# A decoder on one core: the second cross attention's outputs are finished a batch later, and the feed-forward weights are loaded and summed during it

## The chip, the cores and the metric

The kernel runs on one core of a Trainium2 chip. The metric is the device time of one execution in microseconds (us), less is better. PE is TensorE, DVE is VectorE, ACT is ScalarE, POOL is GpSimd, and SP is the engine whose queue issues all DMA transfers here. Each engine runs its own instruction stream in order; streams meet only at semaphores.

## The reference, cut to what matters

Six layers run one after the other on x of 32 batches x 256 tokens x 256 features, all float32, each followed by a residual addition and a layer norm. The change is in the last two:

```python
# 5: cross attention to ctx (32 x 77 x 256), 16 heads of 16
Q = _split_heads(query @ Wq.T + bq)
K = _split_heads(key @ Wk.T + bk)
V = _split_heads(value @ Wv.T + bv)
attn = jax.nn.softmax(jnp.einsum('bhqd,bhkd->bhqk', Q, K) / jnp.sqrt(jnp.float32(HEAD_DIM)), axis=-1)
out = jnp.einsum('bhqk,bhkd->bhqd', attn, V).transpose(0, 2, 1, 3).reshape(B, S, H * Dh)
x = _layernorm(x + (out @ Wo.T + bo))
# 6: feed-forward with ternary weights and 8-bit activations, inner width 1024
scale = 1.0 / jnp.clip(jnp.mean(jnp.abs(w)), 1e-05)              # of each weight matrix
wq = jnp.clip(jnp.round(w * scale), -1.0, 1.0) / scale
gate = jax.nn.silu(_bitlinear(x, w_gate)); up = _bitlinear(x, w_up)
x = _layernorm(x + _bitlinear(gate * up, w_down))
```

So the scale of a weight matrix needs the sum of the absolute values of all its elements before one element can be rounded.

## The kernel before, in words

`decoder` runs six stages in a row. Each opens a `Stage`, which allocates its buffers and semaphores, writes one instruction stream per engine, and ends with a barrier of all engines; a stage's last store has to land before the next stage starts. Results go through DRAM between stages (`act`).

**`cross_attention_in_halves`** (stage "xa", the second use of cross attention; the first is another function and unchanged) works through 32 batches. A batch has four units u = 0..3, (token tile t, head half c) with 8 heads x 77 context positions = 616 columns each. For each unit PE makes scores, DVE takes maxima (L1597) and subtracts (L1598), ACT takes exponentials (`expo`, L1416), DVE sums and takes the reciprocal (`sums`, L1605 and L1606), POOL multiplies (`divide`, L1513), PE transposes (`turn`, L1294), ACT copies back (`turned`, L1421), PE multiplies by the values (`values`, L1312), ACT copies (`copy_o`, L1426), PE projects (`project_out`, L1322), DVE adds the residual (`residual`, L1632) and takes moments (`moments`), POOL makes the reciprocal deviation (`rstd_of`), and ACT writes y (`finish`, L1470).

The order on every engine is written by hand in a function `batch(this, nxt, after, before, two_before)` for each engine: while batch n is in the middle, n+1 (`nxt`) has its tokens, context, q, k and v prepared, n+2 (`after`) has its tokens transposed (`turn_x` on PE, `copy_x` L1379 on ACT), n-1 (`before`) is projected and gets its residual, and n-2 (`two_before`) is finished. PE's `turn_ctx` of the next batch (L1242) waits for `copy_x`, because both use one PSUM bank. On ACT the second part of a batch reads

```python
turned(j, b, 2)
if nxt is not None:
    expo(*nxt, 0)
if two_before is not None:
    finish(*two_before)
if nxt is not None:
    expo(*nxt, 1)
turned(j, b, 3)
if after is not None:
    copy_x(*after)
```

`in_turns` groups the batches into 8 turns of 4: turn 0 and turn 7 are written out in Python, turns 1 to 6 are a hardware loop (`Fori`) in which waits use register arithmetic.

SP issues, for each batch, a context load, then `spread_v` (12 small transfers, L1189, that put v of the next batch into block form, after PE has used the buffer), then the store of batch n-2, then the token load of batch n+3. Before the first batch it issues nine loads of constants and weights, and only then tokens and context; ACT, PE, POOL and DVE wait for all nine.

**`bit_ffn`** (stage "ff") handles 64 tiles of 128 tokens. Its SP stream first loads three weight matrices of 1 MB each, then eight batches of tokens. DVE sums the absolute values of each matrix (L3337), PE adds the sums over partitions (L3193), DVE makes means and reciprocals, scales each matrix with the rounding constant added (L3343), clips each (L3346), and ACT takes the constant off into bf16 (L3244). Only after the third matrix do ACT and PE begin on tiles: `top_x` on DVE (L3298), `scale_x` on ACT (L3217), `turn_x` on PE (L3166), `copy_x` on ACT, `project` gate and up on PE (L3150), `gate` with Silu on ACT (L3204), and `hidden` on DVE (L3306), then the down projection. A slot holds steps of seven neighbouring tiles; four slots, -4 to -1, fill the pipeline ahead of the first tile.

## Time and profile before

| | |
|---|---|
| runs | 3952.51 us median of 3 (3949.82 to 3957.18) |
| profiled execution | 3951.09 us, of which the span of instructions is 3949.3 |
| granted PE clock, mean | 0.949 |
| busy, share of span | PE 85%, DVE 80%, ACT 70%, POOL 66% |
| second cross attention | from 3154.3 to 3596.6, and the landing of its last store |
| feed-forward | from 3599.95 to the end |

Times are in us from the start of the span unless marked ns. A busy share over the whole span mixes six stages; what an edit is worth is read within its stage. L numbers are lines of the kernel before.

### The profile page before, as it was taken

To read this page: it belongs to the slowest core of one execution; us is meant where nothing else is said; L and a number is where in the kernel's file an instruction comes from. 1 tells how busy PE (TensorE), PEld (TensorE's weight loads), DVE (VectorE), ACT (ScalarE), POOL (GpSimd) and SP (SyncE) were. 2 spreads that over 40 slices of the span, in tenths; PEclk is the share of its full clock that TensorE was granted. 3 is DMA by queue.
4 is the path that set the end of the run, shared out by engine and by line. 5 is a ranking of instruction groups with operands and counts; after the bars stand their busy time and mean duration, and the time that the engine had idled before them with its cause. 6 is when DMAs were issued, how large, how long until landed. Compare 5 with 4: busy or idle time off the path is not lost. (4 is left out here: it accounts for less than half of the span.)

```text
span 3949.3 us, 73650 instructions
## 1 busy us (share of the span) xinstructions
PE 3345.9 (85%) x22560; PEld 2485.9 (63%) x22592; DVE 3175.4 (80%) x5288; ACT 2773.6 (70%) x5060; POOL 2619.9 (66%) x2794
## 2 busy tenths in 40 slices
PE   8996999979953788888888888888898789994887
PEld 5664666667442567766766777667677567773554
DVE  5665888855395789898898989888898679996998
ACT  2223777744475888888888888888788457774777
POOL 1223677630094799899898999989899646662555
PEclk9997999979987899999999999999999889997999
DMA  2111212142213111111111111111111112222111
GB/s 63 54 53 51 49 47 51 46 100 41 47 43 83 33 50 54 56 53 50 53 49 52 54 56 55 48 52 47 53 49 50 49 48 53 51 54 75 54 59 38
DMA packets 284832, 209.68 MB, mean 53 GB/s; under 512 B 131208, under 2 KB 249544, under 8 KB 284504
## 3 DMA queue, kind: packets, MB, share of 16 engines
q1 hardware_dynamic: 284504, 205.72, 18.8%
q8 instruction: 155, 2.54, 0.3%
q14 instruction: 173, 1.42, 0.1%
HBM read 149.18 MB, written 51.41 MB: 51 GB/s over the span
## 5 line engine op out<-in xcount | busy, mean ns | idle before, releaser
L2817 POOL TENSOR_TENSOR ma_ch<-ma_h,ma_crep 128x512 f32<-128x512 f32 x1024 | 1369.7, 1360 | 169.3 <-DVE ma_h L2919 154.6
L2919 DVE TENSOR_TENSOR_SCAN ma_h<-ma_a,ma_pbu 128x512 f32<-128x512 f32 x1024 | 1213.3, 1206 | 187.6 <-PE ma_pbu L2497 131.7
L2497 PE MATMUL ma_pbu<-ma_ident,ma_bu 128*128 128x128 f32 x4096 | 661.1, 285 | 202.7 <-DVE ma_h L2919 159.7
L2497 PEld LDWEIGHTS ma_pbu<-ma_ident,ma_bu 128*128 128x128 f32 x4096 | 480.1, 145 | 442.9 <-DVE ma_h L2919 315.1
L2704 ACT ACTIVATE ma_a<-ma_dt,ma_A 128x510 f32<-128x510 f32 x1024 | 652.9, 716 | 2.3 <-issue 1.4
L2506 PE MATMUL ma_py<-ma_ident,ma_ch 128*128 128x128 f32 x4096 | 626.9, 279 | 0.8 <-POOL ma_ch L2817 0.8
L2695 ACT ACTIVATE ma_bu<-ma_uT,ma_b_t 128x512 f32<-128x512 f32 x784 | 507.7, 717 | 19.4 <-PE ma_pbu L2497 17.6
L2506 PEld LDWEIGHTS ma_py<-ma_ident,ma_ch 128*128 128x128 f32 x4096 | 497.0, 145 | 6.2 <-issue 3.6
L881 POOL TENSOR_TENSOR xa_prob<-xa_e,xa_rec_head 128x616 f32<-128x616 f32 x128 | 153.2, 1217 | 120.5 <-DVE xa_rec_head L971 120.4
L1513 POOL TENSOR_TENSOR xa_prob<-xa_e,xa_rec_head 128x616 f32<-128x616 f32 x128 | 155.6, 1217 | 91.8 <-DVE xa_rec_head L1606 91.2
L337 POOL TENSOR_TENSOR la_veps<-la_mv,la_eps 128x2 f32<-128x2 f32 x32 | 6.3, 196 | 251.5 <-DVE la_mv L370 251.5
L2180 POOL MEMSET scatter_eps<- 128x4 f32 x1 | 0.1, 102 | 238.9 <-POOLq L40 238.9
L962 DVE TENSOR_REDUCE xa_top<-xa_pS 128x8 f32<-128x616 f32 x128 | 100.4, 784 | 52.2 <-PE xa_pS L650 50.8
L2824 POOL TENSOR_TENSOR ma_bu<-ma_uT,ma_b_t 128x512 f32<-128x512 f32 x128 | 139.6, 1091 | 0.0
L2885 DVE SCALAR_TENSOR_TENSOR ma_xc<-ma_pm,ma_conv,ma_xc 128x510 f32<-128x510 f32 x183 | 133.5, 729 | 7.6 <-ACT ma_xc L2640 5.4
L2541 PE MATMUL ma_pm<-ma_wout,ma_one_av 128*128 128x256 f32 x512 | 134.0, 386 | 0.0
L2452 PE MATMUL ma_pm<-ma_win,ma_xnT 128*128 128x512 f32 x240 | 124.4, 600 | 0.0
L2829 POOL TENSOR_TENSOR ma_dt<-ma_dt,ma_gT 128x512 f32<-128x512 f32 x64 | 99.3, 1553 | 36.2 <-DVE ma_gT L2909 36.2
L1605 DVE TENSOR_REDUCE xa_esum<-xa_e 128x8 f32<-128x616 f32 x128 | 100.8, 788 | 25.7 <-ACT xa_e L1416 19.5
L245 PE MATMUL la_pK<-la_wkv,la_xT 128*128 128x512 f32 x256 | 120.9, 595 | 0.0
L785 ACT ACTIVATE xa_e<-xa_low 128x616 f32<-128x616 f32 x128 | 92.5, 722 | 36.5 <-DVE xa_low L963 36.5
L790 ACT ACTIVATE xa_eT<-xa_pE 128x384 f32<-128x384 f32 (+1 forms) x256 | 98.7, 444 | 27.5 <-PE xa_pE L661 27.4
(368 smaller groups left out, 8026.7 us busy)
## 6 DMA issues: line engine op xcount, KB each, us to landing
ma_crep<-ma_ct_dram SPq DMA_DIRECT2D x256, 256.0 KB, 3.2
xa_x<-act SPq DMA_DIRECT2D x64, 256.0 KB, 2.9
act<-xa_y SPq DMA_DIRECT2D x64, 256.0 KB, 2.1
la_x<-in_x SPq DMA_DIRECT2D x32, 256.0 KB, 2.7
act<-la_y SPq DMA_DIRECT2D x32, 256.0 KB, 2.2
ea_x<-act SPq DMA_DIRECT2D x32, 256.0 KB, 11.3
act<-ea_x SPq DMA_DIRECT2D x32, 256.0 KB, 4.0
ma_x<-act SPq DMA_DIRECT2D x16, 512.0 KB, 4.6
```

The source lines that it names most:

```text
L881: pool.tensor_tensor(prob[:, u % 2, 0:HC * CTX].rearrange("p (h s) -> p h s", h=HC), e[:, u % 2].rearrange("p (h s) -> p h s", h=HC), rec_ ...
L1513: pool.tensor_tensor(prob[:, u % 2, 0:HC * CTX].rearrange("p (h s) -> p h s", h=HC), e[:, u % 2].rearrange("p (h s) -> p h s", h=HC), rec_ ...
L2452: last = pe.matmul(pm[1][:, :], xnT[:, c, t * P:(t + 1) * P], win[:, c, DI:2 * DI], start=(c == 0), stop=(c == C - 1))
L2497: last = pe.transpose(pbu[c % 2][:, t * P:(t + 1) * P], bu[:, s % 2, t, c * P:(c + 1) * P], ident[:, :])
L2506: last = pe.matmul(py[:, t, c * P:(c + 1) * P], ch[:, s % 2, c, t * P:(t + 1) * P], ident[:, :], start=(s == 0 and c == 0), stop=(s == N - ...
L2541: last = pe.matmul(out, yv[:, c, t * P:(t + 1) * P], wout[:, c, :], start=False, stop=(c == IC - 1))
L2695: last = act.activation(bu[:, s % 2, t, :], uT[:, par, t, :], ACT.Copy, scale=b_t[:, par, t, s:s + 1])
L2704: act.activation(a[:, s % 2, c, :].rearrange("p (b t) -> p b t", b=GB)[:, :, 1:S], dt[:, par, c, :].rearrange("p (b t) -> p b t", b=GB)[:, ...
L2817: pool.tensor_tensor(ch[:, s % 2, c], h[:, s % 2, c], crep[:, s % 4, :], ALU.mult).then_inc(multiplied, 1)
L2824: pool.tensor_tensor(bu[:, s % 2, t, :], uT[:, par, t, :], b_t[:, par, t, s:s + 1].broadcast_to([P, DI]), ALU.mult).then_inc(pool_tile_rea ...
L2885: last = dve.scalar_tensor_tensor(out=out[:, :, k:S], in0=src[:, :, 0:S - k], scalar=conv[:, f, 3 - k:4 - k], in1=out[:, :, k:S], op0=ALU. ...
L2919: dve.tensor_tensor_scan(out=h[:, s % 2, c, :], data0=a[:, s % 2, c, :], data1=pbu[c % 2][:, :], initial=0.0, op0=ALU.mult, op1=ALU.add).t ...
```

## The change

Four things are edited.

1. In the second cross attention `finish` handles the batch three back (`three_before`), between `copy_o` of the batch before and `copy_o` of this one; `add_bias` on POOL is done for this batch at the start of `batch` and no longer for the next one in its middle; on SP the token load comes ahead of the store, and the store is of n-3.
2. Its start: tokens of batch 0, identity and head columns are loaded first, then context 0, then the weights. DVE's memsets no longer wait for weights, and ACT's and POOL's waits stand later or are dropped.
3. A new outer stage "fw" holds identity, weights and sums of the feed-forward. SP loads them in 13 pieces (64 KB, then twelve of 256 KB), one after the store in each of batches 4 to 16; DVE sums the three matrices at the end of the attention stage.
4. In the feed-forward the loads and sums are gone from the start; the four leading slots are interleaved with scaling, clipping and rounding of one matrix after the other; PE waits for each matrix at its first use; a one-column Silu comes first on ACT.

```diff
+class FeedForwardWeights:
+    def __init__(self, st, wgu_d, wd_d, ident_d):
...
+        self.pieces = [(self.ident[:, :], ident_d)]
+        for m in range(2):
+            up = wgu_d[m].rearrange("(c p) i -> p c i", p=P)
+            self.pieces += [(self.wgu_f[:, m, c, i:i + 512], up[:, c, i:i + 512]) for c in range(C) for i in range(0, I, 512)]
+        self.pieces += [(self.wd_f[:, c:c + 2, :], down[:, c:c + 2, :]) for c in range(0, I // P, 2)]
...
@@ cross_attention_in_halves @@
-            in_turns(eng, batch, B // 4, 4, (0, 1, 2, -1, -2), link)
+            in_turns(eng, batch, B // 4, 4, (0, 1, 2, -1, -2, -3), link)
@@ sync @@
-            for dst, src in loads:
-                sp.dma_start(dst, src).then_inc(w_loaded, 16)
...
-            for n in range(4):
+            load_x(0, 0)
+            for dst, src in first_loads:
+                sp.dma_start(dst, src).then_inc(i_loaded, 16)
+            load_ctx(0)
+            for dst, src in loads:
+                sp.dma_start(dst, src).then_inc(w_loaded, 16)
+            for n in range(1, 4):
                 load_x(n, n)
                 load_ctx(n)
...
-                if n >= 2:
-                    store(n - 2)
                 if n >= 1 and n + 3 < B:
                     sp.wait_ge(res_added, n)
                     load_x((n + 3) % 4, n + 3)
-            store(B - 2)
-            store(B - 1)
+                if n >= 3:
+                    store(n - 3)
+                if ffn_weights is not None and 4 <= n < 4 + len(ffn_weights.pieces):
+                    sp.dma_start(*ffn_weights.pieces[n - 4]).then_inc(f_loaded, 16)
+            for n in (3, 2, 1):
+                store(B - n)
@@ scalar: batch @@
                 if before is not None:
                     copy_o(*before, 1)
+                if three_before is not None:
+                    finish(*three_before)
                 copy_o(j, b, 0)
                 turned(j, b, 2)
                 if nxt is not None:
                     expo(*nxt, 0)
-                if two_before is not None:
-                    finish(*two_before)
...
             batches(act, batch)
+            finish(last_batch[0], last_batch[1] - 2)
             copy_o(*last_batch, 1)
@@ gpsimd: batch @@
+                add_bias(*this)
                 if nxt is not None:
                     spread_k(*nxt)
...
                 if nxt is not None:
-                    add_bias(*nxt)
                     divide(*nxt, 0)
                     divide(*nxt, 1)
@@ vector @@
+                if nxt is None:
+                    weight_sums(0)
                 if before is not None:
                     residual(*before)
...
+            def weight_sums(m):
+                if ffn_weights is not None:
+                    dve.wait_ge(f_loaded, 16 * len(ffn_weights.pieces))
+                    dve.tensor_reduce(ffn_weights.wsum[:, m:m + 1], ffn_weights.whole(m), AX.X, ALU.add, apply_absolute_value=True)
...
-            dve.wait_ge(w_loaded, 16 * len(loads))
-            dve.tensor_tensor(head_of_two[:, :], head_of[:, 0:2], head_of[:, 2:4], ALU.add)
...
-            link(dve.memset(v_blocks[:, :, :, :, :, :], 0.0))
+            dve.memset(v_blocks[:, :, :, :, :, :], 0.0)
+            dve.wait_ge(i_loaded, 16 * len(first_loads))
+            link(dve.tensor_tensor(head_of_two[:, :], head_of[:, 0:2], head_of[:, 2:4], ALU.add))
...
             moments(last_batch[0], last_batch[1] - 1)
+            weight_sums(1)
             residual(*last_batch)
             moments(*last_batch)
+            weight_sums(2)
@@ bit_ffn: scalar @@
+            def weight(m):
+                w, q = weights[m]
                 act.wait_ge(w_clipped, m + 1)
-                last = act.activation(q, w, ACT.Copy, bias=-ROUND)
-            last.then_inc(setup_done, 1)
+                act.activation(q, w, ACT.Copy, bias=-ROUND).then_inc(w_ready, 1)
+
+            act.activation(warm[:, :], wsum[:, 0:1], ACT.Silu)
             act.sem_inc(g_ready, 1)
+            weight(0)
+            lead(slot, -4, -3, -2)
+            weight(1)
+            lead(slot, -1)
+            weight(2)
             tiles(act, slot)
@@ bit_ffn: vector @@
-            dve.wait_ge(w_loaded, 64)
-            for m, (w, _) in enumerate(weights):
-                last = dve.tensor_reduce(wsum[:, m:m + 1], w, AX.X, ALU.add, apply_absolute_value=True)
...
+            weight(0)
+            lead(slot, -4, -3)
+            weight(1)
+            lead(slot, -2, -1)
+            weight(2)
             tiles(dve, slot, link)
```

## Rows read from the trace of the kernel before

**Rows 1.** Busy time of each engine in a steady stretch: PE, PEld, DVE, ACT, POOL, clock.

```profile
3250.00:3328.00 78.00, 74.03 (x722) 56.91 (x722) 70.39 (x135) 59.07 (x154) 49.59 (x67) 1.00 0.22 53
```

**Rows 2.** Waits over 20 batches (3250 to 3510): us in total, times, longest.

```profile
PE xa_pG L1242 <- ACT xa_xT L1379: 11.5, 20, 0.6
```

**Rows 3.** Timeline of one batch in the hardware loop: start, us, engine, what.

```profile
3357.32 0.80 DVE L1597 TENSOR_REDUCE xa_top<-xa_pS 128x8 f32<-128x616 f32 x1 [0.20 <-PE xa_pS L1283]
...
3358.37 0.38 ACT L1426 ACTIVATE xa_oT<-xa_pG 128x256 f32<-128x256 f32 x1 [1.54 <-PE xa_pG L1312]
...
3360.05 1.09 ACT L1470 ACTIVATE xa_y<-xa_r,xa_shift,xa_rstd 128x256 f32<-128x256 f32 x2
...
3361.59 1.22 POOL L1513 TENSOR_TENSOR xa_prob<-xa_e,xa_rec_head 128x616 f32<-128x616 f32 x1 [1.38 <-DVE xa_rec_head L1606]
...
3363.00 0.35 PE L1242 MATMUL xa_pG<-xa_ident,xa_cx 77*128 77x77 f32 x2 [0.58 <-ACT xa_xT L1379]
...
3363.19 0.76 PE L1294 MATMUL xa_pE<-xa_ident,xa_prob 128*128 128x128 f32 x5
...
3366.44 0.85 POOL L1523 TENSOR_TENSOR xa_kheads<-xa_kT,xa_head_of_two 128x154 f32<-128x154 f32 x2 [1.71 <-ACT xa_kT L1400]
...
3367.82 0.45 SPq L1172 DMA_DIRECT2D xa_cx<-in_ctx  x1
...
3369.22 10.21 SPq L1189 DMA_DIRECT2D xa_v_blocks<-xa_v  x12
...
3370.04 0.80 DVE L1597 TENSOR_REDUCE xa_top<-xa_pS 128x8 f32<-128x616 f32 x1 [0.20 <-PE xa_pS L1283]
```

**Rows 4.** Timeline, DVE's first maximum in batches 1 and 2, before any finish.

```profile
3205.55 0.80 DVE L1597 TENSOR_REDUCE xa_top<-xa_pS 128x8 f32<-128x616 f32 x1 [0.95 <-PE xa_pS L1283]
...
3217.69 0.80 DVE L1597 TENSOR_REDUCE xa_top<-xa_pS 128x8 f32<-128x616 f32 x1
```

**Rows 5.** Timeline, the same instruction in two batches of the last turn.

```profile
3547.54 0.80 DVE L1597 TENSOR_REDUCE xa_top<-xa_pS 128x8 f32<-128x616 f32 x1
...
3560.19 0.80 DVE L1597 TENSOR_REDUCE xa_top<-xa_pS 128x8 f32<-128x616 f32 x1
```

**Rows 6.** Timeline of the end of the attention: last values and a residual.

```profile
3583.51 1.09 PE L1312 MATMUL xa_pG<-xa_eT,xa_v_blocks 128*32 128x256 f32 x16 [1.65 <-DMA xa_v_blocks<-xa_v]
...
3587.07 0.69 DVE L1632 TENSOR_TENSOR xa_r<-xa_pG,xa_x 128x512 f32<-128x512 f32 x1 [2.56 <-PE xa_pG L1322]
```

**Rows 7.** Timeline of the start of the attention, PE's first instruction.

```profile
3164.17 0.66 PE L1356 MATMUL xa_pG<-xa_ident,xa_bv 128*128 128x128 f32 x2 [16.38 <-DVEq L1658]
```

**Rows 8.** Timeline of the start of the feed-forward.

```profile
3599.95 0.35 SPq L3125 DMA_DIRECT2D ff_ident<-in_ident  x1
...
3615.99 2.27 DVE L3337 TENSOR_REDUCE ff_wsum<-ff_wd_f 128x1 f32<-128x2048 f32 x1
...
3619.35 2.48 DVE L3343 TENSOR_SCALAR ff_wgu_f<-ff_wgu_f,ff_wscale 128x2048 f32<-128x2048 f32 x2
...
3624.32 3.71 ACT L3244 ACTIVATE ff_wgu<-ff_wgu_f 128x2048 bf16<-128x2048 f32 x2 [27.68 <-DVE ff_wgu_f L3346]
...
3626.47 0.68 DVE L3298 TENSOR_REDUCE ff_xtop<-ff_x 128x2 f32<-128x512 f32 x1
...
3629.74 0.89 ACT L3217 ACTIVATE ff_xr<-ff_x,ff_xscale 128x256 f32<-128x256 f32 x2
...
3634.23 1.91 PE L3150 MATMUL ff_pup<-ff_wgu,ff_xT 128*128 128x512 bf16 x4
...
3634.52 1.28 ACT L3204 ACT_TABLE_LOAD   x1 [2.03 <-PE ff_pgate L3150]
...
3636.96 1.28 DVE L3306 SCALAR_TENSOR_TENSOR ff_h<-ff_pup,ff_fgu,ff_g 128x1024 f32<-128x1024 f32 x1 [8.42 <-ACT ff_g L3204]
```

**Rows 9.** DMA issues from 3154 to 3640: count, KB each, us to landing.

```profile
xa_x<-act SPq DMA_DIRECT2D x32, 256.0 KB, 2.9
...
ff_x<-act SPq DMA_DIRECT2D x8, 256.0 KB, 7.1
```

More of the change, by code:

```diff
@@ L1324, in project_out, with batch @@
                 last.then_inc(proj_made, 1)
-            def batch(this, nxt, after, before, two_before):
+            def batch(this, nxt, after, before, two_before, three_before):
                 j, b = this
@@ L1426, in copy_o, with batch @@
                 act.activation(oT[:, b % 2, c, :], pG[1][:, 0:S], ACT.Copy).then_inc(oT_ready, 1)
-            def batch(this, nxt, after, before, two_before):
+            def batch(this, nxt, after, before, two_before, three_before):
                 j, b = this
@@ L1437, in batch @@
                 turned(j, b, 1)
+                if normed and nxt is not None:
+                    copy_q(*nxt)
                 expo(j, b, 3)
-                if nxt is not None:
+                if not normed and nxt is not None:
                     copy_q(*nxt)
@@ L1451, in batch @@
                 if nxt is not None:
+                    expo(*nxt, 0)
+                if not normed and nxt is not None:
                     expo(*nxt, 1)
@@ L1455, in batch @@
                     copy_x(*after)
+                if normed and nxt is not None:
+                    expo(*nxt, 1)
             def norm_apply(j, b):
@@ L1531, in add_bias, with batch @@
                 pool.tensor_tensor(x[:, b], x[:, b], bo[:, :].unsqueeze(1).broadcast_to([P, T, D]), ALU.add).then_inc(bias_added, 1)
-            def batch(this, nxt, after, before, two_before):
+            def batch(this, nxt, after, before, two_before, three_before):
+                add_bias(*this)
                 if nxt is not None:
@@ L1536, in batch @@
                 divide(*this, 2)
-                divide(*this, 3)
                 if after is not None and normed:
                     norm_scale(*after)
+                divide(*this, 3)
                 if two_before is not None:
@@ L1606, in sums, with batch @@
                 dve.reciprocal(rec_head[:, u, :], esum[:, u % 2, :]).then_inc(rec_head_ready, 1)
-            def batch(this, nxt, after, before, two_before):
+            def batch(this, nxt, after, before, two_before, three_before):
                 unit(*this, 2)
@@ L1611, in batch @@
                 sums(*this, 2)
-                sums(*this, 3)
                 if after is not None and normed:
                     norm_stats(*after)
+                sums(*this, 3)
                 if two_before is not None:
@@ L1659, in _ @@
             if bv_d is not None:
+                dve.wait_ge(w_loaded, 16 * len(loads))
                 dve.wait_ge(bv_made, 1)
@@ L3095, in bit_ffn, with lead @@
         AROUND = (-2, -1, 0, 1, 2, 3, 4)
+        def lead(slot, *slots):
+            for n in slots:
+                slot(n % 2, *[divmod(n + d, BT) if n + d >= 0 else None for d in AROUND])
         def tiles(eng, slot, link=None):
[L3098 to L3099 removed]
             def step(*around):
@@ L3145, in _, with is_first @@
         def _(pe):
+            def is_first(tile):
+                return type(tile[0]) is int and tile == (0, 0)
             def project(tile, m, out, done):
                 k = tile[1]
+                if is_first(tile):
+                    pe.wait_ge(w_ready, m + 1)
                 for half in range(2):
@@ L3157, in down @@
                 pe.wait_ge(res_added, count(tile))
+                if is_first(tile):
+                    pe.wait_ge(w_ready, 3)
                 for c in range(IC):
```

87 lines of the change are left out of this document (44 added, 43 removed).

## The prediction

> **What bounds the kernel now.** The busy times by stretch come first, then the waits of the second cross attention, then one batch of it in order of time, and last the two ends of that stage. In its steady stretch PE is busy 74.0 of 78 us at the full granted clock [rows 1], DVE 70.4 of 78; nothing else is close. PE's only regular wait there is in front of `turn_ctx`, for ScalarE's `copy_x`: 20 times in 20 batches, 11.5 us on PE, 0.58 each [rows 2, 3]. Follow the batch in [rows 3]: ScalarE runs `finish` (two instructions, 1.09 us, at 3360.05) between the two exponentials of the next batch; the second exponential, the copies of unit 3 and `copy_x` are queued behind it, and PE waits for `copy_x`. Over 15 batches the period is (3547.54 - 3357.32) / 15 = 12.68 us [rows 3, 5].
>
> The trace holds its own experiment. Between batches 1 and 2 there is no finish yet while everything else runs, and the period is 3217.69 - 3205.55 = 12.14 us [rows 4]. Late in the stage, in the turn that is also written out but has finishes, it is 12.65 [rows 5]. So a finish where it stands costs 0.51 us a batch in written-out code.
>
> The second place is the start of the feed-forward stage: from its first instruction at 3599.95 to the first `hidden` at 3636.96, 37.0 us in which DVE waits for 3 MB of weights, then sums, scales and clips all three before anything of a tile runs [rows 8].
>
> **The change, steady part.** `finish` moves a batch later, behind `copy_o(before, 1)`. There ScalarE sits idle 1.54 us for PE's values [rows 3]; 1.09 fit, with 0.45 left. What it needs (rstd, a free y buffer) is a batch old, and `residual` of the same batch, which now needs it, comes on DVE behind the sums that release the divide at 3361.59, 3 us later. What was behind it moves up 0.5 us. What is late next: PE's step after `turn_ctx` is the first transposes of unit 0, which wait for GpSimd's `divide`. That is a loop of its own: DVE's first maximum at 3357.32 to the end of the divide at 3361.59 + 1.22 = 3362.81, plus 0.05, is 5.54; from the transposes at 3363.19 to DVE's next first maximum at 3370.04 is 6.85; together 12.39 [rows 3]. So in the hardware loop the period can fall from 12.68 to 12.39, 0.29 a batch, not the 0.51 of written-out code. The loop holds 24 batches: 24 x 0.29 = 7.0. Of the written-out batches 2, 3, 28 and 29 save 0.51 each: 2.0. Batch 30's finish saves nothing, since PE's last first-half values wait for the spread of v [rows 6], which starts behind batch 30's second-half values and takes the same 10.2 us. Sum 9.0. Bounds: DVE waits only 0.20 a batch for PE at its first maximum [rows 3]; if nothing else of its chain gives way, the loop gains that, 24 x 0.20 + 2.0 = 6.8. If all of PE's 0.58 goes but a hand-over of 0.13, it is 24 x 0.45 + 2.0 = 12.8.
>
> `add_bias` of the same batch in front of `spread_k` costs nothing: GpSimd sits idle 1.71 us there [rows 3], the addition is one instruction of about 1.3 us (an estimate from the divide of 616 columns in 1.22 against its 512 with two inputs), and the key heads that it could delay are ready at 3367.3, some 2 us before PE's scores that end just ahead of the maximum at 3370.04. `load_x` ahead of the store costs nothing either: both of their waits are over before the spread is issued.
>
> The 13 pieces of weights go on SP's queue, one a batch. SP's period is full: the spread takes 10.21, store, tokens and context end at 3368.27, and the next spread starts at 3369.22, 0.95 idle, so the three take 12.73 - 10.21 - 0.95 = 1.57 [rows 3]. Period down 0.29, a piece at the price of the neighbouring issue with its gap, 0.5: 0.16 is left. A spread that starts a little late does no harm either: it is issued to the end 10.21 us after its start and lands about 1 us later (an estimate), some 11.2, and PE wants the blocks a period and one set of scores after the start, some 13.1: 2 us to spare. Price 0; bounds 0 and, see the rival, far more.
>
> The Trainium skill, "DMA: Bandwidth & Descriptors", section on bandwidth, speaks against this edit: batch transfers to 1 MiB or more, each one carries some 2.0 us of fixed cost. The trace has 256 KB loads landing 2.9 us after issue [rows 9], which agrees with such a fixed part. By that rule twelve pieces cost some 24 us more of latency than three big ones would, and it lies beside 13 batches of computing, so the sum is the same by both as long as nobody waits.
>
> **End of the attention.** Each sum of absolute values is one DVE reduction of 2.27 us [rows 8]. The first stands before the residual of batch 30, where DVE is idle 2.56 for PE's projection [rows 6]; the second before that of 31, which waits for values, copy and projection in a row, a longer chain than 30's; the third beside GpSimd's and ScalarE's last finish and the landing of the last store. Taken at 0; uncovered they would cost 2.27 each, and the first has only 0.29 to spare. In the tail ScalarE gets one more finish (1.09), between the last copies of unit 3 and `copy_o` of 31, which waits for PE's last values: 0.
>
> **Start of the attention.** PE now starts at 3164.17, behind a memset of `v_blocks` that itself waited for all weights [rows 7]. The memsets go ahead of the wait; but one token load and one context load go ahead of the weights, about 1 us of transfer. I take 0.5 less, bounds 0 and 0.8.
>
> **Start of the feed-forward.** Weights and sums are there, so the chain from t = 0 (3599.95) is: from the sums' end at 3618.26 to the first scaling at 3619.35 is 1.1 (totals, mean, reciprocal), plus 0.3 for the memset of ones: 1.4. Scale and clip of one matrix, 1.24 each by the pair at 2.48: 3.9. Maximum of the first batch, 0.68 and about 0.4 for two small ones: 5.0; its tokens, issued at 0, land at 2.9 [rows 9]. ScalarE's rounding of the first matrix, 1.86, from 3.95 to 5.8 [rows 8]. From there the order is that of before: `scale_x` at 3629.74, transposes, `copy_x`, gate and up matmuls up to 3634.23 + 1.91 = 3636.14, which is 6.4 [rows 8]; ScalarE's second matrix (1.86) lies beside the gate matmuls of 1.8, and the Silu table load of 1.28, in this path before, is done early by `warm`. First `hidden` at 5.85 + 6.5 = 12.3 instead of 37.0: 24.7 less. The third matrix (1.86 on ScalarE) delays gate 1 to 15.4, so `hidden` of tile 1 comes 3.1 behind tile 0 and tile 2 some 7.1 behind; before, tile 2 came 7.05 behind, so nothing is given back. Bounds 23 and 26: one rounding pass more or less on the path, and the hand-overs, which I took at 0.05 to 0.1. From there the tiles run as before.
>
> One more: the outer stage that holds the weights ends with a barrier of its own. Between the last store's landing and the next stage's first instruction lies about 1.1 us, which holds all of a stage's exit; taken at 0.5, bounds 0 and 1.2.
>
> **Sum.** 9.0 + 0.5 + 24.7 - 0.5 = 33.7 us less. The profiled execution took 3951.09 (span 3949.3 and 1.8 around it): 3917.4. The median of the runs is 1.4 above it: 3918.8.
>
> **Rivals.**
> (1) The moved finish buys nothing: another wait takes its place, DVE's above all, which is busy 90% and has a chain of its own from maximum to maximum. For it: 70.4 of 78. Against: the 12.14 us period carried the same DVE work. Then the sum is 33.7 - 9.0 = 24.7 less: 3927.8.
> (2) The hardware loop gains as written-out code does, because the divide moves up with the rest: 28 x 0.51 = 14.3 instead of 9.0: 3913.5. For it: the period of 12.14 is what the same instructions can do. Against: in the loop transposes to maximum takes 6.85.
> (3) The weight pieces hold up SP and the spreads behind them. If the queue stood for a piece until it has landed, 2.9, SP's period would be 10.2 + 1.6 + 2.9 = 14.7 against 12.4, and 2.3 x 13 = 30 us are lost: 3949, no change. If a piece takes as long as the eight token loads behind the weights do now, 7.1 us [rows 9], the spread behind it is late by 7.1 - 2.2 of slack = 4.9, 64 us over 13 pieces: 3983. It decides for slower from (33.7 + 7.9) / 13 = 3.2 us a piece beyond the slack. Against: SP issues the context load of its period in 0.45 [rows 3], and a load that is alone lands in 2.9. [...]
> (4) The change does only half of what it says at the hand-over, a weight sum or a rounding pass standing in the path: 4 to 6 us more, 3924.
>
> **How the numbers follow.** Forecast 0.66; (1) 0.13; (2) 0.10; (3) 0.03, two thirds of it slower; (4) 0.08. Own range of the forecast from the bounds: 6.8 + 0 + 23 - 1.2 = 28.6 less, to 12.8 + 0.8 + 26 = 39.6 less: 3913 to 3924. With the rivals' times, 3911 to 3928. A measurement of this kernel tells about 0.2%, 7.9 us, from no change. All but (3) are faster by more: 0.96 faster, 0.02 same, 0.02 slower.
>
> **What the profile would show.** The wait of `turn_ctx` for `copy_x` falls from 0.58 to 0.1 to 0.3, PE now waits for `xa_prob` at the first transposes, and the period is 12.4; with 12.68 the step is wrong. `xa_y` on ScalarE lies before the first `xa_oT` of a batch without shifting it. SP shows a piece of some 0.5 us and spreads that start at most 0.2 late. First `ff_h` 12 to 13 us behind the stage's first instruction, with the table load at its start. The prediction is wrong if PE waits for `xa_v_blocks` in batches 5 to 17, or if DVE's residuals of 30 and 31 move.

## The result, and the profile after

The changed kernel takes 3919.64 us (median of 4 runs, 3913.01 to 3921.47), the kernel before 3951.16 (4 runs, 3947.52 to 3957.18): a ratio of 0.9916, 95% interval 0.9898 to 0.9933. Forecast were 3918.8, range 3911 to 3928. The profiled execution took 3920.81, its span is 3919.0. PEld in the rows is PE's loading of matrix operands, which runs beside its matmuls; a wait put down to "issue" is time in which the engine waited for nothing that the profile shows. In what follows L numbers of after and of the experiments are those of their own kernels.

**The page of after**, span and busy time of each engine:

```profile
span 3919.0 us, 73680 instructions
...
PE 3353.1 (86%) x22560; PEld 2492.9 (64%) x22592; DVE 3177.0 (81%) x5288; ACT 2773.0 (71%) x5061; POOL 2620.1 (67%) x2794
```

**After, busy time in the same steady stretch** as [rows 1] (PE, PEld, DVE, ACT, POOL, clock, DMA share, GB/s):

```profile
3250.00:3328.00 78.00, 76.16 (x735) 58.53 (x735) 72.16 (x139) 60.61 (x159) 51.81 (x71) 1.00 0.28 71
```

PE is now busy 76.2 of 78 instead of 74.0; DMA rises from 0.22 to 0.28; e3 below, which has the shorter batch but no pieces, shows 0.25, so half of the rise is the pieces. **After, waits over 20 batches** (3250 to 3498; us in total, times, longest), the answer to [rows 2]:

```profile
PEld xa_pE L1323 <- issue: 13.4, 41, 0.4
...
PEld xa_pG L1271 <- ACT xa_xT L1408: 6.2, 20, 0.3
...
DVE xa_top L1629 <- issue: 1.7, 5, 0.4
```

Before, the same wait of PEld was (3250 to 3510)

```profile
PEld xa_pG L1242 <- ACT xa_xT L1379: 16.1, 20, 0.8
```

The wait of `turn_ctx` for `copy_x` has fallen from 0.80 to 0.31 a batch on PEld; on PE itself it was 0.58 [rows 2], and after shows none of 0.15 us or more. **After, timeline of one batch**, the answer to [rows 3]:

```profile
3355.96 0.80 DVE L1629 TENSOR_REDUCE xa_top<-xa_pS 128x8 f32<-128x616 f32 x1
...
3357.02 0.38 ACT L1455 ACTIVATE xa_oT<-xa_pG 128x256 f32<-128x256 f32 x1 [0.56 <-PE xa_pG L1341]
...
3359.87 0.20 DVE L1638 RECIPROCAL xa_rec_head<-xa_esum 128x8 f32<-128x8 f32 x1
...
3360.24 1.22 POOL L1546 TENSOR_TENSOR xa_prob<-xa_e,xa_rec_head 128x616 f32<-128x616 f32 x1 [2.48 <-DVE xa_rec_head L1638]
...
3361.58 0.53 PEld L1323 LDWEIGHTS xa_pE<-xa_ident,xa_prob 128*128 128x128 f32 x5 [0.24 <-issue]
...
3361.59 0.76 PE L1323 MATMUL xa_pE<-xa_ident,xa_prob 128*128 128x128 f32 x5
...
3367.74 1.08 ACT L1503 ACTIVATE xa_y<-xa_r,xa_shift,xa_rstd 128x256 f32<-128x256 f32 x2
...
3368.32 0.80 DVE L1629 TENSOR_REDUCE xa_top<-xa_pS 128x8 f32<-128x616 f32 x1
```

The period is 3368.32 - 3355.96 = 12.36, and its two halves are those of the prediction: from the maximum to the end of the divide 3361.46 - 3355.96 = 5.50, from the transposes to the next maximum 6.73. ScalarE's `xa_y` now stands a good moment ahead of `xa_oT`, whose idle time fell from 1.54 to 0.56: the finish lies in what was idle. The first maximum of DVE no longer waits.

This batch stands for two in four only. A turn of the hardware loop holds four batches, and over the loop the intervals from first maximum to first maximum repeat with the turn (batches 20 to 24 in each kernel; e9 and e11 are experiments below):

| interval | after | e9, short divide | e11, written out |
|---|---|---|---|
| 20 to 21 | 12.60 | 12.60 | 12.14 |
| 21 to 22 | 12.33 | 12.20 | 12.14 |
| 22 to 23 | 12.36 | 12.21 | 12.46 |
| 23 to 24 | 12.22 | 12.08 | 12.14 |

From the first maximum to the transposes behind the divide all four of after take 5.6; what differs is the way from there to the next maximum, 6.99, 6.75, 6.74 and 6.60 (means over batches 8 to 27). In the long one DVE stands idle some 0.34 ahead of its third maximum for nothing that the profile shows, once a turn (the line `DVE xa_top` of the waits above, 5 times in 20 batches), and the scores come as much later.

**After, the end of the attention and the start of the feed-forward**, the answer to [rows 6] and [rows 8]:

```profile
3576.18 1.09 PE L1341 MATMUL xa_pG<-xa_eT,xa_v_blocks 128*32 128x256 f32 x16 [1.64 <-DMA xa_v_blocks<-xa_v]
3577.09 2.25 DVE L1663 TENSOR_REDUCE fw_wsum<-fw_wgu_f 128x1 f32<-128x2048 f32 x1
3579.74 0.69 DVE L1671 TENSOR_TENSOR xa_r<-xa_pG,xa_x 128x512 f32<-128x512 f32 x1 [0.39 <-PE xa_pG L1351]
...
3584.67 0.69 DVE L1671 TENSOR_TENSOR xa_r<-xa_pG,xa_x 128x512 f32<-128x512 f32 x1 [0.88 <-PE xa_pG L1351]
...
3592.56 3.96 SPq L3165 DMA_DIRECT2D ff_x<-act  x8
...
3592.57 1.28 ACT L3293 ACT_TABLE_LOAD   x1 [3.41 <-PEq L40]
...
3594.33 1.29 DVE L3390 TENSOR_SCALAR fw_wgu_f<-fw_wgu_f,ff_wscale 128x2048 f32<-128x2048 f32 x1 [0.34 <-DVE ff_wscale L3397]
...
3605.36 1.28 DVE L3360 SCALAR_TENSOR_TENSOR ff_h<-ff_pup,ff_fgu,ff_g 128x1024 f32<-128x1024 f32 x1 [1.59 <-PE ff_pup L3193]
...
3609.32 1.28 DVE L3360 SCALAR_TENSOR_TENSOR ff_h<-ff_pup,ff_fgu,ff_g 128x1024 f32<-128x1024 f32 x1
```

The first `hidden` comes 3605.36 - 3592.56 = 12.80 us behind the stage's first instruction, where it was 37.01. Of the 2.56 us that DVE was idle ahead of the residual of batch 30, 0.39 are left beside a sum of 2.25: the sums are inside the idle time.

Where the 30.3 us of the two spans come from (each worked out from the starts of the same instructions in both traces, in us; a minus is time gained):

| stretch | before | after | difference |
|---|---|---|---|
| stages ahead of it, unchanged | 3154.3 | 3156.0 | +1.7 |
| attention: first instruction to first maximum | 24.53 | 24.97 | +0.4 |
| first maximum of batch 0 to that of batch 31 | 393.96 | 384.50 | -9.46 |
| that to the end of the last y | 23.81 | 23.65 | -0.16 |
| to the feed-forward's first instruction | 3.31 | 3.41 | +0.1 |
| to its first `hidden` | 37.01 | 12.80 | -24.21 |
| first to last `hidden` | 295.55 | 296.56 | +1.0 |
| to the end | 16.79 | 17.07 | +0.3 |

So the two mechanisms are 9.5 and 24.2; all the rest together is +3.4, of which 1.7 lie in stages that nobody edited.

### The profile page after: what moved, and what is told of

Its sections match the earlier page's. It is cut to its first block and busy times, and to the rows that moved or that the text cites. A ratio compares the mean times of both kernels' runs of the same rounds, so it can differ in the third digit from the quotient of the medians.

```text
span 3919.0 us, 73680 instructions
## 1 busy us (share of the span) xinstructions
PE 3353.1 (86%) x22560; PEld 2492.9 (64%) x22592; DVE 3177.0 (81%) x5288; ACT 2773.0 (71%) x5061; POOL 2620.1 (67%) x2794
## 5 line engine op out<-in xcount | busy, mean ns | idle before, releaser
L807 ACT ACTIVATE xa_e<-xa_low 128x616 f32<-128x616 f32 x128 | 92.4, 722 | 36.7 <-DVE xa_low L985 36.7
L1445 ACT ACTIVATE xa_e<-xa_low 128x616 f32<-128x616 f32 x128 | 92.2, 720 | 36.3 <-DVE xa_low L1630 36.3
```

## The experiments

Eleven edited kernels ran, and the changed kernel once more (e12). The ratios of e1 to e12 are to runs of before beside them (medians 3953.3 to 3954.6). Total times of several have wide intervals against effects of a few us, so each verdict is read from the stretch of the trace that the edit touches, and the time stands beside it. "Loop" is the mean period of batches 4 to 27, "attention" runs from the stage's first instruction to the end of its last y, "first hidden" is counted from the feed-forward's first instruction.

| kernel | loop | attention | first hidden | span | time, us | ratio to before |
|---|---|---|---|---|---|---|
| before | 12.69 | 442.3 | 37.0 | 3949.3 | 3951.16 | |
| after | 12.37 | 433.1 | 12.8 | 3919.0 | 3919.64 | 0.9916 |
| after, run again with e11 | 12.37 | 432.5 | 12.6 | 3914.9 | 3922.37 (3916.71 to 3928.6) | 0.9921 [0.9908, 0.9935] |
| e1 finish back | 12.69 | 442.3 | 12.8 | 3928.7 | 3927.54 (3925.2 to 3930.55) | 0.9930 [0.9913, 0.9946] |
| e2 finish alone | 12.36 | 432.4 | 36.6 | 3933.6 | 3946.06 (3933.23 to 3983.12) | 0.9989 [0.9967, 1.0012] |
| e3 old feed-forward | 12.36 | 432.1 | 36.5 | 3936.9 | 3944.02 (3937.77 to 3949.12) | 0.9977 [0.9966, 0.9987] |
| e4 twice the pieces | 12.64 | 439.4 | 12.8 | 3925.6 | 3926.27 (3924.85 to 3931.09) | 0.9930 [0.9914, 0.9947] |
| e5 three big pieces | 12.37 | 433.1 | 12.8 | 3924.3 | 3925.95 (one) | |
| e6 written out | 12.34 | 432.5 | 12.8 | 3922.3 | 3926.15 (3924.61 to 3928.93) | 0.9934 [0.9917, 0.9950] |
| e7 no early Silu | 12.37 | 433.0 | 13.3 | 3926.9 | 3928.69 (one) | |
| e8 short moments | 12.37 | 432.7 | 12.8 | 3921.6 | 3923.38 (one) | |
| e9 short divide | 12.31 | 430.7 | 12.8 | 3922.5 | 3924.32 (one) | |
| e10 bias back | 12.37 | 432.4 | 12.7 | 3921.7 | 3923.47 (one) | |
| e11 written out, pieces spaced | 12.15 | 428.4 | 12.8 | 3911.4 | 3919.21 (3914.18 to 3921.96) | 0.9912 [0.9897, 0.9927] |

**The finish put back, e1.** After, with `finish` where it was on ScalarE; the order of loads and stores stays new.

```diff
@@ scalar: batch @@
-                if three_before is not None:
-                    finish(*three_before)
...
                     expo(*nxt, 0)
+                if two_before is not None:
+                    finish(*two_before)
...
-            finish(last_batch[0], last_batch[1] - 2)
```

> The changed kernel with `finish` alone put back between the two exponentials of the next batch. Theory (the moved finish gives the steady gain): the period returns from 12.38 to 12.68 us in the loop, from 12.14 to 12.65 in written-out batches, the attention stage is 9 us longer, the time 3929. Rival (the new order of loads, bias and stores gives it): the period stays at 12.4 and the time at 3920.

The 128 maxima of this kernel (count; ns least, median, most; first and last start):

```profile
L1628 DVE TENSOR_REDUCE xa_top<-xa_pS x128: 746/789/801, 3181.0 to 3582.2; 128x8 f32<-128x616 f32 x128
```

From the first to the last are 401.2 us, as before (3178.9 to 3580.1); the loop is back at 12.69 and the attention at 442.3. Every us of the loop's gain hangs on the place of this one call.

**The finish moved alone, e2.** Before, with the finish a batch later and the store of n-3 behind the token load; nothing else.

```diff
+                if three_before is not None:
+                    finish(*three_before)
                 copy_o(j, b, 0)
                 turned(j, b, 2)
                 if nxt is not None:
                     expo(*nxt, 0)
-                if two_before is not None:
-                    finish(*two_before)
...
```

> The kernel before with `finish` moved a batch later, and nothing else but the stores of n-3 and the token load ahead of them. Theory: period 12.38, 9 us less than before, 3942. Rival (it needs the freed middle of GpSimd's batch, where the bias addition stood): the gain is half or less, 3946 or more. The spread of v should start 0.1 us behind PE's values in every batch, since SP has no weight pieces.

```profile
L1598 DVE TENSOR_REDUCE xa_top<-xa_pS x128: 745/787/801, 3173.2 to 3564.8; 128x8 f32<-128x616 f32 x128
```

391.6 us, against 391.8 after (3181.0 to 3572.8) and 401.2 before; the attention is 9.9 shorter. The loop runs at 12.36 without a piece in it. The time of this kernel scattered from 3933 to 3983 and settles nothing; the trace does.

**Attention of after, feed-forward of before, e3.** The attention stage neither loads nor sums weights; the feed-forward does both at its start, as before, and the outer stage is gone.

```diff
@@ decoder @@
-        with Stage(nc, "fw") as fw:
-            ffn_weights = FeedForwardWeights(fw, a["L1_ffn_wguT"], a["L1_ffn_wdT"], a["ident"])
...
+    if STAGES > 5:
+        bit_ffn(nc, acts[5], acts[6], a["L1_ffn_wguT"], a["L1_ffn_wdT"], a["ident"])
...
```

> The changed attention with the feed-forward as before: no weight pieces, no sums in the attention, 3 MB of weights loaded and summed at the start of the feed-forward. Theory: first `hidden` is 37.0 us behind the stage's first instruction again instead of 12.8, so 24 us more than the changed kernel, 3944; the attention stage keeps its 9 us and SP's queue has slack again. Rival (the pieces slow the attention): the attention stage is also shorter than in the changed kernel, by up to 2 us.

The first `hidden` is back at 36.5. Here the weights' part of the attention is missing, and the attention is 1.0 us shorter than after and 0.4 shorter than in the second run of after. From the first maximum of batch 0 to that of batch 31 it takes 384.2 against 384.5 and 384.0, so most of that lies in the stage's start, which the pieces don't touch. So pieces and sums together cost at most 1 us there and give 23.7 to 24.2 at the next stage's start.

**Twice the pieces, e4.** 25 pieces, 24 of them 128 KB, two a batch from batch 4 on.

```diff
-  ... up[:, c, i:i + 512]) for c in range(C) for i in range(0, I, 512)]
+  ... up[:, c, i:i + 256]) for c in range(C) for i in range(0, I, 256)]
...
-                if ffn_weights is not None and 4 <= n < 4 + len(ffn_weights.pieces):
-                    sp.dma_start(*ffn_weights.pieces[n - 4]).then_inc(f_loaded, 16)
+                if ffn_weights is not None and n >= 4:
+                    for piece in ffn_weights.pieces[2 * (n - 4):2 * (n - 4) + 2]:
+                        sp.dma_start(*piece).then_inc(f_loaded, 16)
```

> The changed kernel with each weight piece cut in two, so 25 transfers of half the size, two in each of batches 4 to 16. The same bytes, 12 issues of 0.5 us more on SP. Theory A (SP's issue time is full with one piece: in the profile of the changed kernel its period is 12.39 to 12.44 in those batches and the spread starts up to 1.4 us behind PE's values): the period there becomes 12.9, the lag passes the 2 us that the blocks have in hand after 2 to 4 batches, PE then waits for `xa_v_blocks`, and the stage is 13 x 0.5 - 2 = 4 to 5 us longer. Theory B (the lag is the transfers', not the issue's): same bytes, same time.

Its waits from 3200 to 3560, and SP's queue in one batch:

```profile
PE xa_pG L1342 <- DMA xa_v_blocks<-xa_v: 7.7, 11, 1.4
```

```profile
3296.96 10.21 SPq L1210 DMA_DIRECT2D xa_v_blocks<-xa_v  x12
...
3308.28 1.01 SPq L1240 DMA_DIRECT2D fw_wgu_f<-in_L_ffn_wguT  x2
...
3309.85 10.21 SPq L1210 DMA_DIRECT2D xa_v_blocks<-xa_v  x12
```

SP's own period is 12.89, more than the 12.37 of the engines; the spread starts later batch by batch, up to 3.3 us behind PE's use of the buffer, and PE waits for `xa_v_blocks` 11 times. That costs 6.3 us of attention, where 4 to 5 were expected; one single issue that took 1.75 us instead of 0.47 (at 3268.44) accounts for 1.3 of it, and why it did isn't shown. The same bytes cost nothing in 13 issues and 6.3 us in 25: what a piece takes from the attention is issue time on SP.

**SP's queue after.** With one piece the same view of after reads

```profile
3355.99 10.21 SPq L1210 DMA_DIRECT2D xa_v_blocks<-xa_v  x12
3366.24 0.52 SPq L1190 DMA_DIRECT2D xa_x<-act  x1
3366.80 0.46 SPq L1200 DMA_DIRECT2D act<-xa_y  x1
3367.31 0.47 SPq L1239 DMA_DIRECT2D fw_wd_f<-in_L_ffn_wdT  x1
3367.82 0.51 SPq L1193 DMA_DIRECT2D xa_cx<-in_ctx  x1
3368.44 10.21 SPq L1210 DMA_DIRECT2D xa_v_blocks<-xa_v  x12
```

Spread to spread are 12.45 against the engines' 12.37: not 0.16 left, but 0.02 to 0.08 too little. Over the 13 batches with a piece the start of the spread slides from 0.14 to 1.37 us behind the end of PE's `values`, and then falls back to 0.14. Some 0.8 of that slide come from two of the spreads, whose issue took 10.6 us instead of 10.2; the rest is the overrun. Slack is what hides it, but there is less than the 2 us of the prediction: where PE has to wait for the blocks (e4), its values start 11.66 to 11.74 us behind the start of the spread; in after they start 12.9 to 13.3 behind it where the spread is on time, and 11.93 at the worst. That is a slack of 1.2 to 1.6, of which 0.3 were left in the worst batch.

**Three big pieces, e5.** One transfer of 1 MB for each matrix.

```diff
-            self.pieces += [(self.wgu_f[:, m, c, i:i + 512], up[:, c, i:i + 512]) for c in range(C) for i in range(0, I, 512)]
+            self.pieces += [(self.wgu_f[:, m], up)]
-        self.pieces += [(self.wd_f[:, c:c + 2, :], down[:, c:c + 2, :]) for c in range(0, I // P, 2)]
+        self.pieces += [(self.wd_f[:, :, :], down)]
```

> The changed kernel with the weights in three transfers of 1 MB (and the identity) in batches 4 to 7, not twelve of 256 KB. Theory: SP issues nine fewer transfers, so its queue lags in four batches only; but a transfer of 1 MB takes some 3 us of all DMA engines, so the spread of v behind it lands later, by about 3 us against 2 in hand: PE waits for `xa_v_blocks` about 1 us in three batches, and the attention is 1 to 3 us longer than with pieces. Rival (bigger transfers are simply better): no wait of PE for `xa_v_blocks`, the attention is 0.5 us shorter, since SP's queue is free again.

433.07 us of attention against 433.12. The spread slides up to 1.87 us, and PE never waits for it. A transfer of 1 MB does hold up the spread behind it (SP's intervals are 12.43, 13.08 and 12.75 there, 12.38 or 12.39 with pieces of 256 KB), but three of them don't use up the slack, and my expectation of 1 to 3 us fell. The rule of the Trainium skill (DMA: Bandwidth & Descriptors, section on bandwidth, transfers of 1 MiB or more) is neither confirmed nor contradicted in price: twelve transfers or three, nobody waits for their latency. The trace has it at 4.0 us a piece, not at the 2.9 of [rows 9]; a piece is the third transfer in a row there, behind a token load and a store. The page of after's transfers (3156 to 3600):

```profile
xa_x<-act SPq DMA_DIRECT2D x32, 256.0 KB, 3.0
act<-xa_y SPq DMA_DIRECT2D x32, 256.0 KB, 3.1
...
fw_wgu_f<-in_L_ffn_wguT SPq DMA_DIRECT2D x8, 256.0 KB, 4.0
```

**Which engine holds the loop at 12.37: e8 and e9.** e8 takes the statistics over 64 of 256 features and leaves the rest out, which takes 0.4 us of DVE out of a batch. e9 divides 4 of the 8 heads of a unit and leaves the other 4 at zero, which makes each GpSimd divide 0.70 instead of 1.22.

```diff
# e8
-                    last = dve.bn_stats(stats[:, p, t, :], r[:, p, t, :])
+                    last = dve.bn_stats(stats[:, p, t, :], r[:, p, t, 0:64])
# e9
-  pool.tensor_tensor(prob[:, u % 2, 0:HC * CTX]..., e[:, u % 2]..., ...)
+  pool.tensor_tensor(prob[:, u % 2, 0:HB * CTX]..., e[:, u % 2, 0:HB * CTX]..., ...)
...
```

> The changed kernel with the statistics of an output row taken over 64 of its 256 features, which takes about 0.4 us off DVE in each batch, at a point that PE and GpSimd don't wait for. Theory (the period of 12.37 in the loop is the round of PE, DVE's maxima and first sums, GpSimd's first divide, and PE): DVE gets idle time before its first maximum and the period stays 12.37. Rival (DVE's own chain of work is the bound, it has no idle time before the first maximum any more): the period falls to about 12.0.

> The changed kernel with GpSimd's divide of each unit over 4 of its 8 heads, the rest left at zero, so 0.6 us instead of 1.22. The companion of the run with the short statistics, where 0.4 us less on DVE left the period at 12.37. Theory (the round through GpSimd's divide is the bound in the loop): the period falls until the next bound, PE's own work with its short waits, about 12.2 in the loop. Rival (the register waits of the loop alone set it): 12.37 stays.

e8's waits from 3250 to 3500:

```profile
DVE xa_top L1629 <- PE xa_pS L1312: 8.6, 20, 0.6
```

The loop stays at 12.37, and DVE now stands idle 0.43 a batch ahead of its first maximum, waiting for PE: what DVE was relieved of came out as idle time. DVE's work as a whole does not bind, though it is busy 72.2 of 78; its maxima and first sums are part of the round. e9 shortens the round through the divide by 0.5, but the loop falls by 0.06 only. In its steady stretch

```profile
3250.00:3328.00 78.00, 76.56 (x753) 59.04 (x752) 72.32 (x140) 61.03 (x160) 38.32 (x69) 1.00 0.28 71
```

PE is busy 76.6 of 78. Two things hide what the divide is worth there. SP's queue becomes late: the spread starts up to 1.9 us behind, and in six of the batches with pieces PE's values start at the 11.66 where they wait for it. And the interval across the turn of the hardware loop does not move. Behind the pieces the table above shows it cleanly: 12.60 stays 12.60, the other three fall by 0.13 to 0.15, the shortest to 12.08, which is PE's own work. PE's busy time per batch is 74.03 / 78 x 12.68 = 12.03 before [rows 1] and 76.16 / 78 x 12.37 = 12.08 after. So after the change the round through the divide holds three of four intervals, by 0.14, though 0.52 were taken from it; then comes PE's own work, 0.3 beneath the mean period. The fourth interval is held by something else in DVE's stream at the turn of the loop. The prediction had the first right and mentioned neither of the others.

**The loop written out, e6 and e11.** The prediction read 12.14 for the written-out batches [rows 4] and 12.39 for the hardware loop. e6 writes all of the attention's turns out in Python; e11 does that and sends a piece only in every second batch (4, 6, ... 28).

```diff
@@ in_turns @@
+    if written:
+        for turn in range(1, turns):
+            for k in range(per):
+                step(*peeled(turn, k))
+        return
# e11 in addition
-                if ffn_weights is not None and 4 <= n < 4 + len(ffn_weights.pieces):
-                    sp.dma_start(*ffn_weights.pieces[n - 4]).then_inc(f_loaded, 16)
+                if ffn_weights is not None and n % 2 == 0 and 4 <= n < 4 + 2 * len(ffn_weights.pieces):
+                    sp.dma_start(*ffn_weights.pieces[(n - 4) // 2]).then_inc(f_loaded, 16)
```

> The changed kernel with all 32 batches of the second attention written out, no hardware loop. Theory (in the loop a batch costs 12.37 because the waits with register arithmetic lengthen the chain; written out it is 12.14): 24 x 0.23 = 5.5 us less in PE's and DVE's chains; but SP's queue with a weight piece needs 12.4 a batch and becomes the pace in batches 4 to 16, which gives back 13 x 0.25 less the 2 us in hand, about 1.5. So the attention is 4 us shorter than in the changed kernel and the time 3916. Rival (a batch in the loop is bound by work, not by its form): 12.37 stays. Another: fetching the longer program stalls the engines, and it is slower.

> All 32 batches written out, and the 13 weight pieces one in every second batch (4, 6, ... 28) instead of one in each of 4 to 16. Theory (written out a batch is 12.14 and SP's 12.4 with a piece was what held it back in the run before): SP averages 12.15, its lag stays under 1 us, no batch waits for `xa_v_blocks`, and from first maximum to last the attention takes 31 intervals of 12.14 with the first at 14.9: 379, which is 5.4 us less than the changed kernel. Rival (the long intervals of the run before came from fetching the longer program): they stay, 384.

e6's waits from 3200 to 3560:

```profile
PEld xa_pG L1346 <- DMA xa_v_blocks<-xa_v: 6.1, 9, 2.4
```

e6's first maximum in batches that follow each other (timeline):

```profile
3347.15 0.80 DVE L1634 TENSOR_REDUCE xa_top<-xa_pS 128x8 f32<-128x616 f32 x1
...
3359.56 0.80 DVE L1634 TENSOR_REDUCE xa_top<-xa_pS 128x8 f32<-128x616 f32 x1
...
3373.89 0.80 DVE L1634 TENSOR_REDUCE xa_top<-xa_pS 128x8 f32<-128x616 f32 x1
```

Most of e6's batches take 12.14, but SP needs about 12.4 with a piece: the spread slides by some 0.24 a batch (0.65 in the first), the slack, which is 1.3 us in written-out code (12.70 - 11.38, counted as for e4 above), is gone at batch 9, and PE waits. The longest interval is 14.33 - 12.14 = 2.2 us over, and 1.6 of that is one issue of a piece (at 3347.27 in SP's timeline) that took 2.09 us where the others take 0.47; no run shows why. Of some 5 us gained by the shorter period 0.6 are left. In e11 the queue recovers in every other batch:

```profile
L1634 DVE TENSOR_REDUCE xa_top<-xa_pS x128: 746/789/801, 3177.6 to 3564.0; 128x8 f32<-128x616 f32 x128
```

386.4 us from the first to the last maximum, against 391.4 in after run beside it; all batches but one take 12.14, and the attention is 428.43 against 432.49, 4.1 less. The loop form costs 0.23 a batch. Where it lies is seen by following the round of one batch of e11 (timeline) beside that of after:

```profile
3353.96 0.20 DVE L1643 RECIPROCAL xa_rec_head<-xa_esum 128x8 f32<-128x8 f32 x1
...
3354.24 1.22 POOL L1551 TENSOR_TENSOR xa_prob<-xa_e,xa_rec_head 128x616 f32<-128x616 f32 x1 [2.49 <-DVE xa_rec_head L1643]
...
3355.51 0.53 PEld L1328 LDWEIGHTS xa_pE<-xa_ident,xa_prob 128*128 128x128 f32 x5
```

The divide starts 3354.24 - 3354.16 = 0.08 behind the end of the reciprocal and the transposes 3355.51 - 3355.46 = 0.05 behind that of the divide. In after the two are 3360.24 - 3360.07 = 0.17 and 3361.58 - 3361.46 = 0.12. The trace of after holds the comparison within itself: in its written-out batches (0 to 3 and 29) they are 0.08 and 0.05 too, in its loop (5 to 27) 0.17 and 0.12 to 0.13. So 0.16 of the loop's price are two hand-overs; the rest lies between the transposes and the next maximum (6.60 to 6.99 against 6.68), the idle time of DVE once a turn above all. A third place says the same of a wait for a DMA: PE's values that wait for the blocks start 11.66 to 11.74 us behind the start of the spread in the loop (e4) and 11.37 to 11.40 in written-out code (e6). That it is the register arithmetic of the waits, and nothing else of the loop's form, is my reading; no run takes the two apart. The 41 issue waits ahead of the transposes in after are no measure of the loop form: e9 runs in the loop and has

```profile
PEld xa_pE L1323 <- issue: 8.2, 20, 0.4
```

The 20 more in after (13.4 us against 8.2 in 3250 to 3498) are short waits for the divide: they go when it is halved. In the whole time e11's 3919.21 and after's 3922.37 on the same chip have intervals that overlap, so it can't be called faster than after; it beats before by as much as after does.

**Small parts, e7 and e10.** e7 drops the early one-column Silu; e10 puts `add_bias` back ahead of the divide.

```diff
# e7
-            act.activation(warm[:, :], wsum[:, 0:1], ACT.Silu)
# e10
-                add_bias(*this)
...
+                    add_bias(*nxt)
                     divide(*nxt, 0)
```

> The changed kernel without the one-column Silu at the start of the feed-forward's ScalarE stream. Theory: the table load of 1.28 us moves back in front of the first `gate`, behind PE's gate matmuls; the up matmuls of 1.9 us end later than the Silu did before, so about 1 us of it shows: first `hidden` 13.3 us behind the stage's start, not 12.8. Rival (it is on no path): 12.8.

> The changed kernel with the bias addition on GpSimd where it stood before the change, ahead of the first divide of the next batch. Theory (it costs nothing in either place: GpSimd waits some 2.4 us for the first sums after it): the attention stays at 433.1 us, period 12.37. Rival (in the shorter batch it would delay the divide that now sets the pace): the period rises by 0.1 or more.

e7's start of the feed-forward (timeline):

```profile
3597.11 3.96 SPq L3165 DMA_DIRECT2D ff_x<-act  x8
...
3607.99 1.28 ACT L3250 ACT_TABLE_LOAD   x1 [0.23 <-PE ff_pgate L3193]
...
3610.43 1.28 DVE L3359 SCALAR_TENSOR_TENSOR ff_h<-ff_pup,ff_fgu,ff_g 128x1024 f32<-128x1024 f32 x1 [2.13 <-ACT ff_g L3250]
```

The table load of 1.28 is back between the gate matmuls and Silu, and the first `hidden` comes at 13.32 instead of 12.80: 0.5 of the 1.28, as the up matmuls cover the rest. The third `hidden` then comes 7.84 behind the first and not 7.04, mostly as PE's up matmuls ahead of it took 1.72 instead of 1.04 us at a granted clock of 0.58 (3616 to 3620; 1.00 in after); with one run of e7, whether the missing Silu has a part in that is open. e10 leaves the loop at 12.37: the new place of `add_bias` is worth nothing, as forecast.

**After a second time, e12**, beside e11, unchanged.

> The changed kernel itself, unaltered, on the same chip as the written-out version: its time there, for a direct comparison. 3920 expected, ratio to before 0.992, and 5 us more than the written-out version with spaced pieces.

Its span is 3914.9, 4.1 less than that of the first profile, and 3.2 of them lie ahead of the attention. Spans of one execution can't tell a few us; stretches within a stage, which agree to about 0.6, can.

## Why the prediction was right, step by step

- **Steady part, forecast 9.0, measured 9.46** (9.2 to 9.9 in e1 and e2). Right, with its mechanism: e1 and e2 tie all of it to the place of `finish`, and the round named is the next bound, halves 5.50 and 6.73 against 5.54 and 6.85. The 24 loop intervals gave 7.7 where 7.0 were forecast (12.69 to 12.37 a batch), the four written-out ones 2.0 as forecast, and the first interval of the stage lost 0.3. How close the period came is in part luck: 12.39 was read from one batch, and 12.37 is the mean of intervals from 12.22 to 12.60, of which the longest is not held by the round at all. Rival (1) is out by e1, e2 and e8, rival (2) by the loop's own period; e11 shows that its 12.14 is real, but not for a hardware loop. What the forecast did not name is how near PE's own work of 12.08 lies, so that a still shorter round would have given little (e9).
- **`add_bias`, new order of loads and stores, forecast 0.** Right (e10, e2).
- **The pieces, forecast 0.** The price is right, at most 1 us by e3, but the step "0.16 is left" failed: SP is 0.02 to 0.08 a batch over its period while pieces last. The subtraction took all 0.95 us between SP's last issue and the next spread as idle; back to back a batch of SP's without a piece takes 11.84 (3428.65 - 3416.81 in after), so 0.06 of it was not to be had, a piece takes 0.54 and not 0.5, and the period is 12.37 where 12.43 was reckoned with. The spreads start up to 1.37 late, not "at most 0.2". The second ground, slack, carried it, 1.2 to 1.6 of it where 2 were worked out. The comparison with three big transfers was miscounted: by the prediction's own 2.0 us, nine transfers more are 18 us of latency, not 24; it enters no sum, and e5 shows no difference. Rival (3) had a real mechanism with a small size: it is issue time, not landing time, and half a microsecond more per batch costs 6.3 us (e4), not 30 or 64.
- **Weight sums, forecast 0 with 0.29 to spare.** 0.39 and 0.88 of idle time were left, the tail is 23.65 against 23.81. Right.
- **Start of the attention, forecast 0.5 less, measured 0.4 more.** PE's first instruction did come 0.32 earlier counted from the stage's start: 9.51 against 9.83 [rows 7]; it now waits for the load of a bias and no longer for DVE. Of that 0.15 were left at the q projection (19.85 against 20.00), and there it was lost, before and after:

```profile
3174.34 2.64 PE L1263 MATMUL xa_pG<-xa_xT,xa_wq 128*128 128x256 f32 x8
```

```profile
3175.88 3.23 PE L1292 MATMUL xa_pG<-xa_xT,xa_wq 128*128 128x256 f32 x8
```

The same eight matmuls took 0.59 longer, at a mean granted clock of 0.58 (3175.88 to 3179.11) where it was 0.71 (3174.34 to 3176.98). In the other kernels they took 2.2 to 3.5. So the first maximum came at 24.97 against 24.53, and in the eleven experiments anywhere from 24.3 to 25.3, e2 with the old order of loads among them at 24.4. A gain of this size is below what the start varies by; the step is mis-sized, its value about 0.
- **Start of the feed-forward, forecast 24.7 less, measured 24.2.** First `hidden` at 12.80 instead of 12.3: I took the hand-overs at 0.05 to 0.1, and DVE alone waited 0.34 for its own `ff_wscale`. "Tile 1 comes 3.1 behind tile 0" was wrong: it is 3.96, as it was before; tile 2 comes 7.04 behind, as forecast. The stretch from the first `hidden` to the last took 1.0 longer than before, 0.5 in e3, which has the old start, and 0.0 in e2. I have no cause for the last 0.5 to 1.0.
- **Outer barrier, forecast 0.5 more.** The end took 0.28 longer, and 3920.81 - 3919.0 = 1.8 lie around the span as before. But e3, which has no outer stage, ends 0.39 later than before too (17.19), and the same code took 16.6 to 17.4 in most kernels and 18.2 to 19.2 in e7, e9 and e11. So no cost of the barrier is seen, and its value is 0 as far as these traces tell.

Sum forecast 33.7; by the trace 30.3, and without the 1.7 of the unchanged stages 32.0. That the median of after lies only 0.8 us from the forecast is luck in part: the two big terms came within 0.5 each, most of the small ones fell short, and the median of before came down by 1.4 with its fourth run (3952.51 to 3951.16).

## What to carry to other kernels

A call that waits for nothing young is best placed where its engine already stands idle; look for a batch of the trace in which that call is missing, for its period tells what moving it is worth. Then ask for the next round that closes (here maximum, divide, transposes, scores) and for the busiest engine's work per period, since the gain stops at the first of them. Count the issue time of a queue against the period, not its DMA share: at 0.28 of DMA share SP's queue was full, and one more issue a batch was hidden only by slack that a longer row of pieces or a shorter period would have used up (0.3 us of it were left). And read a period from a whole turn of a hardware loop, not from one batch of it.

## What was not expected of the hardware

- Where a transfer stands in the queue shows in its landing. A store of 256 KB landed 2.2 us after issue where it was issued ahead of the token load (before), and 3.1 to 3.2 behind it, with weight pieces (after) and without (e2, e3). A piece, third in the row, took 4.0.
- A hardware loop whose waits compute on registers took 12.37 a batch, the same instructions written out 12.14; one hand-over was 0.17 instead of 0.08, the next 0.12 instead of 0.05, and one batch of each turn of four took 12.60.
- Beside transfers of 1 MB the intervals of SP's queue were 12.43, 13.08 and 12.75, beside those of 256 KB of the same matrix 12.38 to 12.39; spreads started up to 1.87 us late with three such transfers and up to 1.37 with twelve of 256 KB.
- Single issues on SP took 1.75 us (e4) and 2.09 (e6) where the other weight pieces took about 0.5. No run shows why.
- In the first batch of the attention the same eight matmuls of the q projection took 2.64 us at a mean granted clock of 0.71 before and 3.23 at 0.58 after; nothing in them was changed.
